# Taking the unread TensorE products out of a two-block MetaFormer kernel, from its router on

## What is computed

```python
x = x + _L0_conv_ref(_ln_c(x), ...)            # 1x1 products, pairwise gram features, 1x1 products
t = _to_tokens(x)
t = t + _L0_ffn_ref(_ln_t(t), ...)             # router: 2 experts of 8 for each image; layer norm at its end
x = _from_tokens(t, x)
x = x + _L1_conv_ref(_ln_c(x), L1_conv_w)      # 3x3 convolution, divided by 9
t = _to_tokens(x)
t = t + _L1_ffn_ref(_ln_t(t), ...)             # gate: 2 experts of 8 for each token, all 8 computed
x = _from_tokens(t, x)
```

## Time and profile before

| | us |
|---|---|
| median of 3 runs | 331.59 |
| lowest, highest | 330.18, 332.70 |
| the profiled execution | 332.67 |
| its span in the profile | 330.9 |
| PE busy | 296.1 |
| DVE, ACT, POOL busy | 161.2, 169.4, 37.8 |

### The profile page before, as it was taken

One profiled execution on the slowest core, in us unless ns is written; L12 is line 12 of the kernel. 1 busy time (PEld: TensorE's weight loads), 2 busy tenths in 40 slices (PEclk: granted clock), 3 DMA queues, 4 the chain that ended last, 5 costly groups with the idle time before them and its releaser, 6 DMA issues.

```text
span 330.9 us, 6793 instructions
## 1 busy us (share of the span) xinstructions
PE 296.1 (90%) x2568; PEld 159.4 (48%) x2568; DVE 161.2 (49%) x378; ACT 169.4 (51%) x328; POOL 37.8 (11%) x78
## 2 busy tenths in 40 slices
PE   3968999799697999899998899999999999999993
PEld 2732534365474456796886434433333333333441
DVE  0425785583641175737775333933344433444433
ACT  3441153315346735525314465566667777777772
POOL 7084074200045000000000000000000000000000
PEclk9995999999787999699979999999999999999999
DMA  7587778880000000000000199300029950610000
GB/s 208 181 186 173 169 167 179 190 283 0 0 2 0 0 3 3 0 2 0 2 0 1 37 216 206 64 2 0 0 53 200 224 110 2 125 35 3 13 22 18
DMA packets 12240, 25.46 MB, mean 77 GB/s; under 512 B 2448, under 2 KB 4656, under 8 KB 12080
## 3 DMA queue, kind: packets, MB, share of 16 engines
q1 hardware_dynamic: 10352, 20.01, 25.9%
q0 software_dynamic: 1536, 4.43, 6.5%
q10 hardware_dynamic: 320, 0.59, 0.6%
HBM read 14.55 MB, written 1.33 MB: 48 GB/s over the span
## 4 chain that ended last, share of the span: by engine, by line
PE 70%; ACT 8%; DVE 6%; DMA 6%; issue 5%; SPq 3%; DVEq 1%; ACTq 0%
PE PS L760 18%; PE PS L738 16%; PE PS L692 7%; DMA moved<-amp 5%; PE PS L482 4%; PE PS L515 4%; SPq L382 3%; PE PS L490 3%; PE PS L569 3%; PE PS L646 3%; PE PS L504 3%; PE PS L664 2%; ACT h L909 2%; DVE D L1233 2%; ACT amp L909 1%
## 5 line engine op out<-in xcount | busy, mean ns | idle before, releaser
L738 PE MATMUL PS<-N,late 64*64 64x512 f32 (+1 forms) x640 | 78.2, 549 | 0.2 <-DVE yraw L1178 0.2
L909 ACT ACTIVATE amp<-PS,late 128x512 f32<-128x512 f32 (+1 forms) x80 | 47.2, 641 | 25.0 <-PE PS L738 24.6
L909 ACT ACTIVATE h<-PS,late 128x512 f32<-128x512 f32 (+1 forms) x80 | 47.2, 641 | 16.7 <-PE PS L738 16.3
L738 PEld LDWEIGHTS PS<-N,late 64*64 64x64 f32 x640 | 26.9, 133 | 33.7 <-issue 31.8
L760 PE MATMUL PS<-h,late 64*64 64x512 f32 (+1 forms) x320 | 39.6, 556 | 2.2 <-DVE D L1233 1.3
L760 PE MATMUL PS<-amp,late 64*64 64x512 f32 (+1 forms) x320 | 39.2, 552 | 0.7 <-ACT amp L909 0.3
L1071 DVE TENSOR_TENSOR h<-moved,amp 128x384 f32<-128x384 f32 x48 | 24.3, 544 | 17.7 <-DMA moved<-amp 8.2
L1233 DVE SCALAR_TENSOR_TENSOR D<-PS,late,moved 128x512 f32<-128x512 f32 (+1 forms) x24 | 14.8, 657 | 35.9 <-PE PS L760 35.9
L1233 DVE SCALAR_TENSOR_TENSOR D<-PS,late,img 128x512 f32<-128x512 f32 x16 | 11.3, 746 | 34.9 <-PE PS L760 30.2
L382 POOL DMA_DIRECT2D moved<-amp x48 | 23.7, 502 | 30.1 <-ACT amp L828 29.6
L692 PE MATMUL PS<-img,conv_hl 128*128 128x288 f32 x144 | 24.8, 337 | 2.2 <-DVE amp L1163 2.2
(11 more groups left out here) (142 smaller groups left out, 319.6 us busy)
## 6 DMA issues: line engine op xcount, KB each, us to landing
moved<-amp SPq DMA_DIRECT2D x48, 96.0 KB, 4.1
img<-gates_hbm SPq DMA_DIRECT2D x4, 1024.0 KB, 13.9
moved<-amp POOLq DMA_DIRECT2D x42, 96.0 KB, 4.3
moved<-gates_hbm SPq DMA_DIRECT2D x4, 512.0 KB, 7.3
moved<-gates_hbm SPq DMA_DIRECT2D x2, 1024.0 KB, 10.0
late<-late_in SPq DMA_DIRECT2D x1, 1852.0 KB, 7.5
moved<-gates_hbm SPq DMA_DIRECT2D x4, 256.0 KB, 4.8
mix<-mix_in SPq DMA_DIRECT2D x1, 897.0 KB, 8.6
```

The source lines that it names most:

```text
L738: mm = pe.matmul(PS[64 * r:64 * r + 64, 2 * (n % RING) + half, 0:w], L("w1")[rows, u:u + 64], N[rows, a:a + w], start=True, stop=True, ski ...
L909: act.activation(hid(n, half)[:, 0:w], PS[:, 2 * (n % RING) + half, 0:w], ACT.Gelu, bias=L("b1")[:, BLOCKS * g + b:BLOCKS * g + b + 1]).th ...
```

## The change

The entries `unread` are taken out of PE's list from `route_logits` on: 12 entries with 34 products. The five entries ahead of it with 16 products stay. No other entry moves, and the lists of ACT and DVE, POOL's and SP's work are the same. The function `unread` is as before.

The core of the diff (two of its rows):

```diff
-        spread 1 3, spread 1 5, route_logits, unread 1, route_loads, route_picks, unread 5, hidden0 0, unread 2, weights, unread 3, bias, unread 3, hidden0 2,
...
-        center 4 2, spread 2 5, center 3 3, root 4 0, center 3 4, center 3 5, root 3 1, unread 4, spread 4 0, unread 4, spread 3 3, spread 4 2, unread 5,
...
+        spread 1 3, spread 1 5, route_logits, route_loads, route_picks, hidden0 0, weights, bias, hidden0 2, hidden0 4, down0 0 0, down0 0 1, hidden0 6,
```

More of the change, by code:

```diff
@@ L174 @@
         products 5 1, spread 1 0, products 5 2, products 5 3, spread 1 2, fc 4, fc 5, center 1 3, center 1 4, center 1 5, root 1 1, root 1 2, unread 2,
-        spread 1 3, spread 1 5, route_logits, unread 1, route_loads, route_picks, unread 5, hidden0 0, unread 2, weights, unread 3, bias, unread 3, hidden0 2,
-        hidden0 4, down0 0 0, down0 0 1, hidden0 6, down0 1 0, down0 1 1, center 2 0, hidden0 8, center 2 1, center 2 2, hidden0 10, root 2 0, hidden0 12,
-        down0 2 0, spread 2 0, down0 2 1, spread 2 2, center 3 0, hidden0 14, center 3 1, center 3 2, unread 4, root 3 0, down0 3 0, down0 3 1, center 2 3,
-        spread 3 0, center 2 4, spread 3 2, center 2 5, unread 1, root 2 1, conv 0, conv 1, conv 2, conv 3, center 4 0, spread 2 3, unread 1, center 4 1,
-        center 4 2, spread 2 5, center 3 3, root 4 0, center 3 4, center 3 5, root 3 1, unread 4, spread 4 0, unread 4, spread 3 3, spread 4 2, unread 5,
-        logits 0, spread 3 5, mix 1, conv 4, mix 1, unread 1, conv 5, turn 0 0, turn 0 1, turn 0 2, conv 6, conv 7, mix 2, center 4 3, center 4 4, center 4 5,
-        mix 1, root 4 1, mix 5, spread 4 3, mix 2, spread 4 5, mix 6, logits 1, mix 8, turn 1 0, mix 7, turn 1 1, mix 8, turn 1 2, mix 119,
+        spread 1 3, spread 1 5, route_logits, route_loads, route_picks, hidden0 0, weights, bias, hidden0 2, hidden0 4, down0 0 0, down0 0 1, hidden0 6,
+        down0 1 0, down0 1 1, center 2 0, hidden0 8, center 2 1, center 2 2, hidden0 10, root 2 0, hidden0 12, down0 2 0, spread 2 0, down0 2 1, spread 2 2,
+        center 3 0, hidden0 14, center 3 1, center 3 2, root 3 0, down0 3 0, down0 3 1, center 2 3, spread 3 0, center 2 4, spread 3 2, center 2 5, root 2 1,
+        conv 0, conv 1, conv 2, conv 3, center 4 0, spread 2 3, center 4 1, center 4 2, spread 2 5, center 3 3, root 4 0, center 3 4, center 3 5, root 3 1,
+        spread 4 0, spread 3 3, spread 4 2, logits 0, spread 3 5, mix 1, conv 4, mix 1, conv 5, turn 0 0, turn 0 1, turn 0 2, conv 6, conv 7, mix 2,
+        center 4 3, center 4 4, center 4 5, mix 1, root 4 1, mix 5, spread 4 3, mix 2, spread 4 5, mix 6, logits 1, mix 8, turn 1 0, mix 7, turn 1 1, mix 8,
+        turn 1 2, mix 119,
     """,
```

## The result

| | before | changed |
|---|---|---|
| median, us | 331.41 (4 runs) | 337.98 (4 runs) |
| lowest, highest | 330.18, 332.70 | 336.77, 340.88 |
| profiled execution | 332.67 | 336.77 |
| its span | 330.9 | 334.9 |

The ratio is 1.0208 with a 95% interval of 1.0159 to 1.0257: slower by 5.3 to 8.5 us; whether it is more or less than 2% stays open.

The account below looks back on a forecast made before the run. TensorE bounds the second mixture, so its start matters. Direct gain -0.6 and clock losses 1.8, 0.8, 0.3, 0.4, 0.5 sum to +3.2 us on the profiled 332.67: 335.9, less 0.4 gives 335.5, range 332 to 339.

Parts of the forecast that it names:

- The direct gains: Time saved by removing the products themselves: 0.6 us in the gate stretch, 0 for all other groups.
- The logits, the spread and the mix step: Gate stretch at half clock: logits +1.8 us, spread 3 5 +0.8, first mix step +0.3.
- Spreads 3 3 and 4 2: Before the logits: 0 if the clock falls after them, +1.2 us if before; +0.4 taken.
- The router term: Low clock of 87.2 to 94 runs on through 100.8, slowing hidden0 and down0 products after it: +0.5 us.
- Conv 4 and after: Conv 4 at half clock already: 0; up to 1.2 us either way by when the clock returns; 0 taken.
- Conv 0 to 3: Gap before 135.5 grows, but the clock fell there already: 0, bounds -1.2 and +1.2 us.
- Clock at half from 94 to 100.8: Sign in the router: granted clock at half there confirms the router term; at full refutes it.
- Logits near 4 us and the fall before 165: Sign in the gate stretch: logits near 4 us instead of 2.14, clock at half before 165, confirm the main term.
- Conv 4 2 to 3 us later: Sign: conv 4 starting 2 to 3 us later than 169.66, second mixture as long as before, confirms the sum.
- ACT's gelus of hidden0 1 and 2 not earlier: Sign in the router: ACT starting them before 99.31 would refute that the router's removed products are hidden.
- The unmoved clock: Rival: same clock falls at the same places, only the direct gain of 0.6 us, 332.1 us; chance 0.15.
- the full 6.8 us: Rival: all removed products in the chain of waits come out, 6.8 us faster, 325.9 us; chance 0.06.
- The spreading case: Rival: half clock also through conv 5, later router, spreads and one further stage: +7.8 us, 340.5 us; chance 0.07.

Follow-up runs that it names:

- thin_gate: The kernel before, with the 13 unread products of the gate stretch kept in number and place but 16 columns wide instead of 128; ratio 1.0171.
- after_3: The changed kernel unaltered, run for a third profile; 333.15 us.
- after_again: The changed kernel unaltered, run once more for a second profile; 340.32 us.
- before_4: The kernel before unaltered, run for a fourth profile, without any clock fall behind the router; 331.23 us.

## Why the prediction was right, and where its sizes were off

**The bound and the direction.** The second mixture, conv 7 to the end, took 146.67 to 146.76 us in every profile, so only its start moved. Behind route_logits the changed kernel took 245.9 us (mean of three) and before 240.6 (mean of five): 5.3 us slower. The stages that grew are those where the clock fell earlier or stayed low longer; all others are the same within 0.2 us. That the width of the products is what held the clock is shown for the gate stretch (thin_gate) and only argued for the router. The time, 337.98, is inside 332 to 339 and 2.5 above the 335.5. Against the median of before, 3.9 us more were forecast and 6.6 measured.

**The direct gains.** Right in the main. The gate stretch gave 0.53 us where 0.6 was counted. Two that were put at 0 were small but not nothing. Without the router's 14 products hidden0 4 comes 13.98 to 14.02 us behind route_logits; with them it comes 13.97 to 13.99 us behind in six profiles, and 14.22 to 14.47 in the four in which the low clock of the router lasted longest (9.5 to 10.1 us), so there they stand in the way. And center 2 0 to root 2 1 is 25.6 us without the four products in it, 25.7 with them. The 6.8 us of the chain were worth 0.5 to 0.8 us: each of its pieces lay beside ACT or DVE work that ended hardly earlier.

**The logits, the spread and the mix step.** 1.8 predicted, 1.85 measured; 0.8 and 0.3 predicted, 1.33 measured together (2.53 to 3.86, means). Spreads 3 3 and 4 2: both bounds came true, 0 in after_3 and about 1 in the other two (7.27 against 6.31). Predicted net of the direct gain -0.2, measured +0.1.

**The router term.** Mis-sized. +0.5 was taken; hidden0 4 to center 2 0 went from 7.65 (mean of five) to 9.11, +1.46. The step that failed is "the clock was low there until 104.3 already": I priced against the fall from 100.8 to 104.3, and this fall is in one execution of five. Against the four others the low clock costs 1.8 us. The bound of 2.1 held.

**Conv 4 and after.** 0 taken, +0.78 measured (13.55 to 14.32, means), by the same error: the fall at 169.1 is in one of five. Conv 0 to 3: 0 taken, +0.03 measured, because there the clock falls in most executions of both.

**The base, and luck.** The sum of 335.9 was made on the first profile, and I took off 0.4 because that profile seemed slow. Three errors partly cancelled. Behind route_logits this profile was the slowest of five, 3.3 us above their mean; the terms, +3.2, were 2.1 too small beside the 5.3 measured; so the sum gave 247.2 there where 245.9 was measured, 1.3 too much. Ahead of it the ramp of 86.94 was one of the shortest, 2.8 below the median of the 14, 89.8. 335.9 - 1.3 + 2.8 = 337.4, beside the measured 337.98. So the direction and the mechanism were earned, and the time came as near as it did partly by luck.

**The signs it named.** Clock at half from 94 to 100.8: yes. Logits near 4 us and the fall before 165: yes, 3.99 and 161.9. Conv 4 2 to 3 us later: it started 85.42 us behind route_logits instead of 82.72, so 2.7, once the ramp is taken out; but by the means of five and three profiles it is 4.5 (80.4 to 84.9), since the first profile of before was late there too. ACT's gelus of hidden0 1 and 2 not earlier: 12.38 us behind route_logits, and 12.37 before.

**The rivals.** The unmoved clock and the full 6.8 us fell by the windows of the changed kernel. The spreading case came in part in after_again, where the low clock ran on to 181. The rule of the Trainium skill (TensorE: Matmul & The Clock Gate, section on HAM oscillation), by which longer idle gaps than these throttle the array, does not account for the falls here: in thin_gate PE has no idle time from 158.45 on, and the clock falls at 161.6 and stays at 1.2 GHz for 17 us. The same page of the Trainium skill remarks, of the start of a kernel (section What's actually happening), that the number of slow matmuls changes from run to run. Later in the kernel the trace has the like: five executions of before had the clock fall again at none, one or three places behind the router.

## What to carry to other kernels

Products that nobody reads are not waste to be cleaned up by the busy row or by the chain of waits: 6.8 us of them stood in the chain, 0.5 to 0.8 us came out, and without all 34 the kernel was 5.3 us slower behind the router. Price them by what the granted clock does to the thin work behind them, and put them ahead of a fall, since behind it they only stood in the way here. And take the profile of before more than once when the clock has edges: a fall that one execution shows is no base to price against.

## What the runs showed of the hardware

- TensorE can be busy throughout and still lose half its clock: in thin_gate it was never idle from 158.45 on, the clock fell at 161.6, and it was busy for 17.00 of 17.00 us at 0.50, with instructions of 16 and 96 columns ahead of the dense ones.
- The same kernel differs between executions by more than this change costs: the 23 runs of before in one session spread from 329.09 to 339.27 us. Behind the router 5.4 us of spread (238.56 to 243.96) lie in where the clock fell and how long it stayed low; ahead of it 4.4 us (86.94 to 91.33) lie in the ramp, whose causes I did not take apart.
- Half clock does not double a convolution product. In the first profile of before, conv 1 starts 4.49 us behind conv 0 (136.93 to 141.42), inside the low stretch of the earlier trace rows; in before_4, at full clock, 2.65 us behind it: a factor of 1.7. The logits, with their 128-column weight loads, took 3.99 us against 2.14, a factor of 1.9.
